# Attention and low-rank gate on one core: the probabilities turned by VectorE squares and DMAs, and mixed two units later

## The reference

```python
xn = layernorm(x)
q, k, v = xn @ Wq.T, xn @ Wk.T, xn @ Wv.T          # heads of 128
q, k = rmsnorm(q, q_norm_w), rmsnorm(k, k_norm_w)
scores = q @ k.T / sqrt(128) + where(rel > 0, -1e30, slope * rel)
s = (softmax(scores) @ v) @ Wo.T
g = silu(2 * sum over 8 experts e of 8 * softmax(xn @ Wr.T + br)[e] * (xn @ A[e].T) @ B[e].T)
y = x + s * g
```

## Time and profile before

| What | Value |
|---|---|
| Time, median of 3 runs | 858.25 us (852.56 to 859.21) |
| Profiled execution, first to last instruction | 856.8 us |
| TensorE busy / VectorE / ScalarE / GpSimd | 824.0 / 655.6 / 446.8 / 197.7 us |
| Mean granted clock of TensorE | 0.990 of full speed |
| Bytes moved by DMA | 28.68 MB |

### The profile page before, as it was taken

How to read it: one execution, slowest core, us unless ns; L and a number is a source line. 1 busy time by engine, 2 the same in 40 slices (tenths; PEclk the granted TensorE clock), 3 DMA queues, 4 the chain that set the end, 5 groups by cost and what they waited for, 6 DMA issues and landing times.

```text
span 856.8 us, 15004 instructions
## 1 busy us (share of the span) xinstructions
PE 824.0 (96%) x4641; PEld 707.6 (83%) x4641; DVE 655.6 (77%) x1716; ACT 446.8 (52%) x1114; POOL 197.7 (23%) x155
## 2 busy tenths in 40 slices
PE   8999999999999999999999999999999999999888
PEld 7788888888887888878887888878888788788776
DVE  6967787778876787777976778767887678878776
ACT  4555455555553554554555455544555356455733
POOL 4310141212222041301403104121222204130253
...
DMA packets 7138, 28.68 MB, mean 33 GB/s; under 512 B 944, under 2 KB 1328, under 8 KB 5168
## 3 DMA queue, kind: packets, MB, share of 16 engines
...
## 4 chain that ended last, share of the span: by engine, by line
PE 82%; DVE 9%; issue 6%; ACT 1%; POOL 1%; DMA 1%; DVEq 0%; SPq 0%; ACTq 0%; POOLq 0%
PE qkv_ps L903 9%; PE qkv_ps L904 9%; PE qkv_ps L905 9%; PE turn_ps L1043 7%; PE out_ps L903 6%; PE out_ps L905 6%; PE out_ps L904 6%; PE score_ps L903 4%; PE mix_ps L903 4%; PE mix_ps L905 4%; PE mix_ps L904 4%; PE score_ps L905 4%; PE score_ps L904 4%; PE turn_ps L1018 3%; DVE probs L712 2%
## 5 line engine op out<-in xcount | busy, mean ns | idle before, releaser
L494 ACT ACTIVATE probs<-probs,neg_max 128x128 f32<-128x128 f32 (+3 forms) x256 | 142.5, 557 | 171.5 <-DVE neg_max L700 170.9
L700 DVE CUSTOM_DVE_ANT_0 probs<-score_ps,cst,slope 128x128 f32<-128x128 f32 (+3 forms) x256 | 138.5, 549 | 106.4 <-PE score_ps L905 61.4
L388 POOL TENSOR_TENSOR inv_rms<-mean_sq,minus_half 128x5 f32<-128x5 f32 x64 | 75.0, 1172 | 593.8 <-DVE mean_sq L739 593.8
L903 PE MATMUL qkv_ps<-w_hi,xt_hi 128*128 128x512 f32 (+1 forms) x512 | 177.0, 346 | 2.6 <-DVE xt_lo L651 1.6
L904 PE MATMUL qkv_ps<-w_lo,xt_hi 128*128 128x512 f32 (+1 forms) x512 | 175.5, 343 | 0.0
L905 PE MATMUL qkv_ps<-w_hi,xt_lo 128*128 128x512 f32 (+1 forms) x512 | 174.7, 341 | 0.0
L526 ACT ACTIVATE pt_hi<-turn_ps 128x512 fp32r<-128x512 f32 x160 | 90.3, 597 | 83.8 <-PE turn_ps L1043 83.8
L759 DVE TENSOR_TENSOR pt_lo<-turn_ps,pt_hi 128x512 fp32r<-128x512 f32 x160 | 106.1, 688 | 23.5 <-ACT pt_hi L526 23.3
L903 PEld LDWEIGHTS qkv_ps<-w_hi,xt_hi 128*128 128x128 f32 x512 | 98.5, 192 | 15.6 <-DVE xt_lo L651 1.9
L904 PEld LDWEIGHTS qkv_ps<-w_lo,xt_hi 128*128 128x128 f32 x512 | 98.4, 192 | 11.7
L905 PEld LDWEIGHTS qkv_ps<-w_hi,xt_lo 128*128 128x128 f32 x512 | 98.0, 191 | 11.9
...
## 6 DMA issues: line engine op xcount, KB each, us to landing
...
x_sb<-x SPq DMA_DIRECT2D x8, 256.0 KB, 6.1
x_sb<-x SPq DMA_DIRECT2D x1, 2048.0 KB, 10.1
y<-acc SPq DMA_DIRECT2D x7, 256.0 KB, 2.0
w_raw<-wqkv SPq DMA_DIRECT2D x4, 384.0 KB, 5.2
...
```

The lines of the kernel that those rows point to most:

```text
L388: nc.gpsimd.tensor_tensor(inv_rms[:, :], mean_sq[:, :], minus_half[:, 0:NORMED], ALU.pow).then_inc(inv_rms_ready, 1)
L494: nc.scalar.activation(probs[:, h, 0:n], probs[:, h, 0:n], ACT.Exp, bias=neg_max[:, h:h + 1], scale=-1.0, accum_out=total[:, h:h + 1]).the ...
L700: nc.vector.tensor_tensor_reduce(probs[:, h, 0:n], score_ps[:, h % 2, 0:n], cst[:, C_DIST + SEQ - n:C_DIST + SEQ], slope[:, h:h + 1], HUGE ...
L903: pe.matmul(out, a_hi, b_hi, start=start, stop=False)
```

## The change

- **Turning.** Probabilities are turned by VectorE in 32x32 squares (`square_probs`: two `STREAM_TRANSPOSE` for a unit, each for two heads) from `probs` to a new tensor `squared`. Sixteen DMAs of 32 partitions each (`move_probs`, SyncE) then put the squares where they belong, from `squared` to `moved`: two buffers, in the space of `x_sb`. Only the last unit (`BY_PE`) is still turned by TensorE.
- **Parts.** `moved_hi` (ScalarE) and `turned_lo` (GpSimd) read `moved` in SBUF; `LO_BY_DVE` is empty, so GpSimd makes all low parts, in its slot ahead of `inverse_rms`.
- **Scaling** of the probabilities is ScalarE's now (256 Copies with a scale); VectorE makes the reciprocals.
- **Order.** `mix` is two units behind the scores (`mix(t-2)` in slot t) and `out` three; both are whole calls. In TensorE's slot the mix stands ahead of q's turn and `project`. `moved_hi(t-1)` stands in ScalarE's slot between the parts of q and k and `square_qk`. GpSimd's and ScalarE's weight pieces are spread over other slots: `split_wo` in slot 2 of a group, the four pieces of `split_w` in slots 5 and 6. SyncE's loads of weights are cut in two or four and stand behind the moves of slots 3, 4, 6 and 7.
- **x again.** `x_sb` is taken by `moved`, so the second load of x goes to `w_raw` and `wo_raw` in the last group.

```diff
+            def move_probs(g, t):
+                i, to = t % QB, moved[t % 2]
+                sp.wait_ge(probs_squared, TWO(g, t, 2))
+                for k in range(QUADS):
+                    for q in range(QUADS):
+                        sp.dma_start(to[k * QUAD:(k + 1) * QUAD, q, 0:(i + 1) * P],
+                                     squared[q * QUAD:(q + 1) * QUAD, k, 0:(i + 1) * P]).then_inc(probs_moved, 16)
...
+            def turned_lo(g, t):
...
+                for j in range(t % QB + 1):
+                    if t % QB < QB - 1 or j not in LO_BY_DVE:
+                        pool.wait_ge(pt_hi_ready, PER_KEY_BLOCK(g, t, j + 1))
+                        nc.gpsimd.tensor_tensor(by_quad(pt_lo, j), moved_block(t, j), by_quad(pt_hi, j).bitcast(F32),
+                                                ALU.subtract).then_inc(pt_lo_by_pool, 1)
...
+            def normalize_probs(g, t, heads):
...
+                act.wait_ge(recip_ready, TWO(g, t, heads[0] // 2 + 1))
+                for h in heads:
+                    nc.scalar.activation(probs[:, h, 0:n], probs[:, h, 0:n], ACT.Copy,
+                                         scale=recip[:, h:h + 1]).then_inc(probs_ready, 1)
...
+            def moved_hi(g, t):
+                act.wait_ge(probs_moved, MOVED(g, t, 16 * QUADS * QUADS))
+                if t > 0:
+                    act.wait_ge(mix_ready, ONE(g, t, 0))
+                for j in range(t % QB + 1):
+                    nc.scalar.activation(by_quad(pt_hi, j), moved_block(t, j), ACT.Copy).then_inc(pt_hi_ready, 1)
...
+            def square_probs(g, t, h):
...
+                dve.wait_ge(probs_ready, PER_HEAD(g, t, h + 2))
+                if t > 0 and h == 0:
+                    dve.wait_ge(probs_moved, MOVED(g, t, 0))
...
             def slot(g, t, left):
-                i = t % QB
                 if t % BLOCKS == 0 and here(t, left):
                     set_slope(g, t)
                 if here(t, left):
-                    for h in range(HPG):
-                        bias(g, t, h)
-                    normalize_probs(g, t)
+                    bias(g, t, 0)
+                    bias(g, t, 1)
+                    reciprocals(g, t, 0)
+                    bias(g, t, 2)
+                    bias(g, t, 3)
+                    if not by_pe(t, left):
+                        square_probs(g, t, 0)
+                if here(t - 3, left) and not (left == 1 and t > BLOCKS):
+                    add_out(g, t - 3, left)
+                if here(t, left):
+                    reciprocals(g, t, 2)
+                if here(t - 2, left) and not by_pe(t - 2, left):
+                    mixed_lo(g, t - 2, left)
+                if here(t, left) and not by_pe(t, left):
+                    square_probs(g, t, 2)
                 if here(t + 1, left):
                     turned_qk_lo(g, t + 1)
...
             def slot(g, t, left):
...
                 if here(t, left):
                     scores(g, t, 0)
...
+                    scores(g, t, 1)
+                if here(t - 3, left) and not (left == 1 and t > BLOCKS):
+                    out(g, t - 3, left)
                 if here(t, left):
                     scores(g, t, 2)
+                    scores(g, t, 3)
+                if here(t - 2, left) and not by_pe(t - 2, left):
+                    mix(g, t - 2, left)
                 if here(t + 1, left):
+                    turn_q(g, t + 1)
                     turn_k(g, t + 1)
...
                 if here(t + 2, left):
+                    project(g, t + 2)
```

More of the change, by code:

```diff
@@ L351, in _ @@
+            sp.wait_ge(xt_turned, BLOCKS)
+            for t in range(3):
+                move_probs(0, t)
+            pipeline(sp, slot)
             for t in range(BLOCKS - 2):
@@ L440, in _ @@
             split_wo(0, range(2, HPG))
+            turned_lo(0, 0)
+            slot(0, 2, GROUPS)
             pipeline(pool, slot)
@@ L541, in slot @@
-                if here(t + 2, left) and not split:
+                if here(t - 1, left) and not by_pe(t - 1, left):
+                    moved_hi(g, t - 1)
+                if here(t + 2, left):
                     square_qk(g, t + 2)
-                if here(t, left):
-                    for j in range(min(2, i + 1)):
-                        turned_hi(g, t, j)
-                if here(t + 2, left):
-                    if split:
-                        square_qk(g, t + 2)
-                        turned_hi(g, t, 2)
-                    value_hi(g, t + 2)
@@ L564, in _ @@
+                if w_due and t % BLOCKS == 5:
+                    split_w(g + 1, range(0, 1))
+                if left == 1:
+                    if t == SILU_SLOT:
+                        gates()
+                    if t == BLOCKS:
+                        for n in range(QB):
+                            turned_hi(n)
+                        mixed_hi(g, BLOCKS - 1, left)
             split_first_w(range(0, 1))
@@ L611, in _ @@
             keep_gate_in(5)
-            mixed_hi(0, 0, GROUPS)
-            for j in range(2):
-                turned_hi(0, 1, j)
             keep_gate_in(6)
             keep_gate_in(7)
+            moved_hi(0, 0)
+            slot(0, 2, GROUPS)
             pipeline(act, slot)
@@ L1078, in out @@
+                last.then_inc(mix_ready, 1)
+            def out(g, u, left):
+                bank = out_bank(u, left)
+                pe.wait_ge(o_lo_ready, ONE(g, u, 1))
+                if not (left == 1 and u == BLOCKS - 2):
+                    pe.wait_ge(acc_ready, 1 + ONE(g, u - 1, 1))
+                for h in range(HPG):
                     if u % BLOCKS == 0:
                         pe.wait_ge(wo_lo_done, (g + u // BLOCKS) * HPG + (h + 1))
-                    last = three(bank, hi[:, h, :], lo[:, h, :], wo_hi[:, h, :], wo_lo[:, h, :], h == 0, h == HPG - 1)
```

427 lines of the change are left out of this document (195 added, 232 removed).

## The result

The changed kernel takes 1,046.3 us (median of 4 runs, 1,042.4 to 1,060.6), the kernel before 858.7 beside it: a ratio of 1.219, 95% interval 1.211 to 1.227. The ratio leaves out the slowest of the four, an execution in a slower state than the others. I had forecast 966 us, 12.5% slower, in a range of 905 to 1,045; it is 21.9% slower. The profiled execution spans 1,042.3 us, where my sum had 965.

The account below looks back on a forecast made before the run. TensorE bound the old kernel; after the change the loop through ScalarE, GpSimd's low parts and `inv_rms` would. Terms 59 + 85.7 + 686.4 + 93.1 + 28.6 = 952.8, clock 12: 965, median 966 us, range 905 to 1045.

Parts of the forecast that it names:

- the moves, booked at 0: SyncE's sixteen issues a unit, at most 0.46 us each plus 2.0 landing: 9.1 us behind the second transpose, just hidden, 0 booked.
- the clock, booked at 12 us: TensorE idles in every slot, so its granted clock falls often; one fall of 1.5 us a group on the path, 12 us.
- TensorE's turns: 624 of 640 turns leave TensorE, 87 us of its 824; its own loop then sets a slot i = 1 at 13.3 us.
- GpSimd's place in the loop: GpSimd's low parts stand ahead of `inv_rms`, which the next first bias needs: slots of 13.2 to 15.1 us, 114.4 a group.
- the rival: Moves show: landing in 5.2 us instead of 2.0, 15.9 us a slot, 1,060 us; decides from 3.6 us of landing; 8 in 100.
- My rival "in every slot": TensorE's clock falls in each of 60 slots, 1.5 us each, instead of one in eight: 1,040 us; 12 in 100.
- GpSimd's hold on `inv`: VectorE's `inv` slowed beside GpSimd's work; goes free except in slots 5 and 6 of the last group, 1.1 us each.
- Start and end: First bias of slot 2 at 59 us; from the last unit's first bias to the end 28.6 us, 20.7 before.

## Why the prediction was wrong

The step that failed is the moves, booked at 0 because the long slot would just hide them; they were not hidden. The jump, not in the sum, and the clock, booked at 12 us, were too small as well. Removing one after the other goes 1,046.3, 1,005.9 (moves), 983.1 (clock), 966.8 (jump): 40, 23 and 16 us. The three hide each other, so these shares belong to this order.

The last time is the forecast to the microsecond, and that is luck. The sum was 952.8 and 12 for the clock; that run spans 962.7, where the start is 2.5 us longer than in the sum, the six groups 4.9 (part of it low clock), the end 2.7. What holds is the terms: slots 2 to 7 of group 0 take 85.7 (85.7), the six groups 691.3 (686.4), the last group to slot 7 93.0 (93.1). In the changed kernel these are 100.8, 741.1 and 105.2.

- **TensorE's turns.** Right: 624 turns went, and TensorE's loop sets slots 1 at 13.1 (13.3).
- **GpSimd's place in the loop.** Right, by its numbers (114.5 to 115.9 against 114.4 a group with the covers off) and by its cause for slots 0, 2, 4 and 7 and in part for 3 (half of the low parts took 34 us off). Single terms: the transpose of 1,024 took 1.25 (1.2), the scaling of 512 on ScalarE 0.72 (0.6; it came out at the exponential's 0.72), `pt_hi` 0.63; in the group shown no slot but 6 (15.2 against 14.5) is off by more than 0.4.
- **The moves "just hidden", booked 0. This step failed.** The term is the interval of the issues. I took at most 0.46 us from three issues in 1.39 at the start; these are 0.62, and 15 x 0.62 + 2.0 + 0.2 = 11.5 instead of 9.1. With that the same reckoning would have shown a wait of 2.5 us in every slot i = 0; it was 2.66 and 3.02. I had also written that the rival decides "from 3.6 us of landing on": the landing was right, at 2.0, and I moved the wrong one of the two numbers. By the same sum it decides from 0.57 us an issue on: 14.3 - 3.6 = 10.7 us, less 2.2, over 15. The rival's 1,060 us is near the result by the wrong term. And I priced the cover in the loop only: in group 0, where unit 2 comes 5.5 us behind unit 1, the moves cost 15 us. Cutting the moves alone took 40 us off.
- **The jump.** Not in the sum. It stood in the trace of before as a bias 3.5 us late with no releaser, six times, where TensorE's bound covered a part of it; I read only its effect on the clock and called it a fall of the clock. In the changed loop the bias stands on the path: 2.4 us in slot 2 of six groups, 14 of the 16 us that writing it out took off. That gain came with the moves out of the way; alone, writing it out gained nothing.
- **The clock, booked at one fall a group, 12 us.** Granted were 0.89 to 0.91 in four slots of eight. Where the fall lies on the path it costs 1.1 (slots i = 0) to 1.5 (i = 1), and up to 0.9 in a slot 6; the extra matmuls took 23 us off with the moves cut and nothing with them in place. My rival "in every slot" was too much, my booking too little: the mean clock of 0.93 does not tell it, the place of each fall does.
- **GpSimd's hold on `inv`.** Small here, as booked, since the low parts stand ahead of `inv_rms`. The run with the other order shows what that place is for. `mean_sq` was hit instead, 0.45 us on average against 0.17.
- **Start and end.** First bias of slot 2 at 60.0 (59). From the last bias to the end 35.3 instead of 28.6: the low parts of unit 62 end 17.6 us behind that bias and not 11.7, for eight additions and products of the last stage (`acc` and `wo_raw`, 1.3 us each) stand ahead of them on GpSimd, and the mix waits for them.

What stays open: why the clock's falls go from one slot to another when the waits change. No run tells what sets the place; they show only that it moves. Open too is what the moves are worth with the other covers gone.
